# Decoder kernel, self attentions and wide cross attention: score matmuls and their PSUM banks rearranged

## What is computed

```python
# layer 1 self attention ("a1"): 16 heads of 8, rotary positions, masked by pages of 32 keys
scores = jnp.einsum('bqhd,bkhd->bhqk', q, k) * scale
scores = jnp.where(allowed[None, None], scores, jnp.finfo(scores.dtype).min)
out = jnp.einsum('bhqk,bkhd->bqhd', softmax(scores), v).reshape(B, T, E) @ wo
# layer 3 self attention ("a3"): 16 heads of 8, no mask, the same form
# layer 3 cross attention ("wide"): 16 heads of 64 over 154 context keys, with masks, then @ WO + bO
```

## Time and profile before

| | |
|---|---|
| median of 3 runs | 2627.68 us (2613.83 to 2633.36) |
| the profiled execution | 2624.98 us |
| its span | 2623.2 us, mean granted clock 0.866 |
| TensorE busy | 80% of the span |
| VectorE busy | 63% |
| ScalarE busy | 39% |

### The profile page before, as it was taken

How to read it: one execution, slowest core, us unless ns; L and a number is a source line. 1 busy time by engine, 2 the same in 40 slices (tenths; PEclk the granted TensorE clock), 3 DMA queues, 4 the chain that set the end, 5 groups by cost and what they waited for, 6 DMA issues and landing times. The chain is left out here.

```text
span 2623.2 us, 35892 instructions
## 1 busy us (share of the span) xinstructions
PE 2103.5 (80%) x11968; PEld 1397.2 (53%) x11992; DVE 1653.1 (63%) x4036; ACT 1028.7 (39%) x2290; POOL 542.7 (21%) x907
## 2 busy tenths in 40 slices
PE   7696999976998796557774995696699878988788
PEld 3354788853555455222332553585343346866677
DVE  5565677764674565569996455456688565555655
ACT  2353222211564452255551343321177633443333
POOL 0341111001110430148882330110211000000000
PEclk8597999986896797679996797798699879999989
DMA  8320000003110420000002310001311100000000
GB/s 316 92 61 16 1 1 1 1 16 106 41 51 21 110 54 1 0 0 1 0 0 88 77 45 7 0 1 42 120 49 41 27 31 1 0 0 0 0 1 17
DMA packets 60049, 94.43 MB, mean 36 GB/s; under 512 B 11313, under 2 KB 33137, under 8 KB 58737
## 3 DMA queue, kind: packets, MB, share of 16 engines
q1 hardware_dynamic: 29792, 55.57, 6.3%
q0 software_dynamic: 29952, 36.45, 5.8%
q10 hardware_dynamic: 144, 0.39, 0.1%
HBM read 65.63 MB, written 31.29 MB: 37 GB/s over the span
## 5 line engine op out<-in xcount | busy, mean ns | idle before, releaser
L904 DVE TENSOR_REDUCE m<-banks 128x1 f32<-128x512 f32 (+3 forms) x512 | 272.4, 583 | 76.7 <-PE banks L1057 50.0
L2435 PEld LDWEIGHTS banks<-w_ffn,eh 128*128 128x128 f32 x2144 | 279.2, 191 | 20.9
L2435 PE MATMUL banks<-w_ffn,eh 128*128 128x128 f32 x2144 | 280.8, 274 | 0.0
L1325 DVE TENSOR_REDUCE m<-banks 128x2 f32<-128x308 f32 x384 | 164.2, 475 | 173.5 <-PE banks L1604 97.9
L1025 ACT ACTIVATE p<-banks 128x512 f32<-128x512 f32 (+3 forms) x512 | 233.9, 522 | 98.4 <-PE banks L1103 58.8
L2423 PE MATMUL banks<-x_hi,w_hi 128*128 128x512 f32 x472 | 210.2, 445 | 18.8 <-PEq L330 18.8
L1055 PE MATMUL banks<-K,Qf 32*128 32x512 f32 (+2 forms) x512 | 180.7, 506 | 37.8 <-PEq L330 32.9
L2424 PE MATMUL banks<-x_lo,w_hi 128*128 128x512 f32 x472 | 188.5, 399 | 0.0
L2425 PE MATMUL banks<-x_hi,w_lo 128*128 128x512 f32 x472 | 187.7, 398 | 0.0
L2405 ACT ACTIVATE et<-banks 128x512 f32<-128x512 f32 x140 | 83.7, 598 | 246.9 <-PE banks L2425 246.9
L1101 PE MATMUL banks<-Q,K 32*128 32x512 f32 (+2 forms) x512 | 151.3, 492 | 15.0 <-ACT p L1025 13.1
(11 more groups left out here) (402 smaller groups left out, 4387.0 us busy)
## 6 DMA issues: line engine op xcount, KB each, us to landing
Qf<-stack_q_plain POOLq DMA_DIRECT2D x48, 256.0 KB, 3.0
Qf<-stack_q_masked POOLq DMA_DIRECT2D x32, 256.0 KB, 3.0
K<-stack_k_self POOLq DMA_DIRECT2D x32, 256.0 KB, 3.1
w_ffn<-ffn_dram SPq DMA_DIRECT2D x1, 6144.0 KB, 36.0
stack_q_plain<-q_hi SPq DMA_DIRECT2D x24, 256.0 KB, 3.5
stack_q_masked<-q_hi SPq DMA_DIRECT2D x16, 256.0 KB, 2.9
stack_k_self<-k_hi SPq DMA_DIRECT2D x16, 256.0 KB, 3.2
K<-stack_k_ctx POOLq DMA_DIRECT2D x48, 80.0 KB, 2.7
```

What stands on the lines that cost most here:

```text
L904: ins = dve.reduce_max(k.m[:, t, h:h + 1], bank[:, 0:(t + 1) * P if k.kind == "page" else S], AX)
L1325: dve.reduce_max(k.m[:, t:t + 2, h], first_banks[c % 3][:].rearrange("p (a k) -> p a k", a=2)[:, :, 0:S2], AX).then_inc(sem("max_done"), 1)
L2435: last = pe.matmul(bank[:, t * P:(t + 1) * P], k.h[:, n % RING, t * P:(t + 1) * P], w(down.format(e))[:, i * P:(i + 1) * P], start=(i == 0 ...
```

## The change

- Self attentions, first scores: banks 2 to 5 as two pairs; two consecutive chunks (two heads) fill a pair, one maximum of 128 x 2 x 512 reads both. TensorE waits once per pair, for the maximum of two pairs before. The result bank moves from 5 to 6.
- Self attentions, second scores: two banks (0, 1) in place of three; unit x waits for the exponential of unit x - 2.
- Wide: `kk` holds each pair of heads once, without zeros; each head has a score matmul of its own over its 64 rows and 154 columns, the two heads of a pair in different banks; both masks after the four matmuls.
- Branches of `narrow_block` that no call reaches are removed.

```diff
-    score_banks, first_banks = tuple(ps[n] for n in SBANKS), tuple(ps[n] for n in FBANKS)
-    o_bank, misc = ps[5], ps[7]
+    score_banks, o_bank, misc = ps[0:2], ps[6], ps[7]
+    def first_pair(pair):
+        at = 2 + 2 * (pair % 2)
+        return net.banks[:, at:at + 2, :]
...
-                bank = first_banks[c % 3]
                 dve.wait_ge(sem("scores_done"), c + 1)
...
-                    ins = dve.reduce_max(k.m[:, t, h:h + 1], bank[:, 0:(t + 1) * P if k.kind == "page" else S], AX)
-                ins.then_inc(sem("max_done"), 1)
+                width = (t + 1) * P if k.kind == "page" else S
+                dve.reduce_max(k.m[:, t, h - 1:h + 1], first_pair(c // 2)[:, :, 0:width], AX).then_inc(sem("max_done"), 1)
...
-                maximum(c)
+                if c % 2 == 1:
+                    maximum(c)
...
-                    nc.scalar.activation(k.p[:, x % PBUFS, q0:S], score_banks[x % 3][:, q0:S], ACT.Exp).then_inc(sem("exp_done"), 1)
+                    nc.scalar.activation(k.p[:, x % PBUFS, q0:S], score_banks[x % 2][:, q0:S], ACT.Exp).then_inc(sem("exp_done"), 1)
...
-                if c >= 3:
-                    pe.wait_ge(sem("max_done"), c - 2)
+                if c >= 4 and c % 2 == 0:
+                    pe.wait_ge(sem("max_done"), c // 2 - 1)
...
-                bank, kt, j = score_banks[x % 3], u // GROUP, u % GROUP
+                bank, kt, j = score_banks[x % 2], u // GROUP, u % GROUP
...
-                if x >= 3:
-                    pe.wait_ge(sem("exp_done"), x - 2)
+                if x >= 2:
+                    pe.wait_ge(sem("exp_done"), x - 1)
...
-        self.kk = sb("kk", [P, HEADS, KPAD])
+        self.kk = sb("kk", [P, HEADS // 2, KPAD])
...
-            dve.memset(k.kk[:], 0.0)
...
-                dve.scalar_tensor_tensor(k.kk[:, 2 * c:2 * c + 2, 0:S2], over(ps[2 + c % 2][:, 0:S2], 1, 2), w("x3_bk")[:, c:c + 1],
-                                         over(w("halfsel"), 2, S2), ALU.add, ALU.mult).then_inc(sem("kk_ready"), 1)
+                dve.tensor_scalar(k.kk[:, c, 0:S2], ps[2 + c % 2][:, 0:S2], w("x3_bk")[:, c:c + 1], None, ALU.add).then_inc(sem("kk_ready"), 1)
...
+                for j in range(GROUP):
+                    c, rows = 2 * g + j // 2, slice(XHD * (j % 2), XHD * (j % 2 + 1))
+                    out = ps[2 * (n % 2) + j % 2][:, j // 2 * S2:(j // 2 + 1) * S2]
+                    pe.matmul(out, k.qT[rows, c, t * P:(t + 1) * P], k.kk[rows, c, 0:S2], start=j < 2, stop=False, skip_group_check=True)
                 for i in range(2):
-                    c = 2 * g + i
                     out = ps[2 * (n % 2) + i][:, 0:2 * S2].rearrange("p (h k) -> p h k", h=2)
-                    pe.matmul(out, k.qT[:, c, t * P:(t + 1) * P], k.kk[:, 2 * c:2 * c + 2, 0:S2], start=True, stop=False)
-                    pe.matmul(out, w("negi"), over(k.mq[:, t, 0:S2], 1, 2), start=False, stop=True).then_inc(sem("scores_done"), 1)
+                    pe.matmul(out, w("negi"), over(k.mq[:, t, 0:S2], 1, 2), start=False, stop=True, skip_group_check=True).then_inc(sem("scores_done"), 1)
```

More of the change, by code:

```diff
@@ L898, in maximum @@
                 h = GROUP * (n % GROUPS) + j
-                bank = first_banks[c % 3]
                 dve.wait_ge(sem("scores_done"), c + 1)
-                if ctx_keys:
-                    ins = dve.reduce_max(k.m[:, t:t + 2, h], bank[:].rearrange("p (a k) -> p a k", a=2)[:, :, 0:S2], AX)
-                else:
-                    ins = dve.reduce_max(k.m[:, t, h:h + 1], bank[:, 0:(t + 1) * P if k.kind == "page" else S], AX)
-                ins.then_inc(sem("max_done"), 1)
+                width = (t + 1) * P if k.kind == "page" else S
+                dve.reduce_max(k.m[:, t, h - 1:h + 1], first_pair(c // 2)[:, :, 0:width], AX).then_inc(sem("max_done"), 1)
             def minus_maxima(n):
-                dve.wait_ge(sem("max_done"), nch * (n + 1))
+                dve.wait_ge(sem("max_done"), nch // 2 * (n + 1))
                 if n >= 2:
@@ L1040, in first_scores @@
                 t, j = k.chunk(i)
-                rows, bank = slice(RG * j, RG * (j + 1)), first_banks[c % 3]
+                rows, bank = slice(RG * j, RG * (j + 1)), first_pair(c // 2)[:, c % 2]
                 if i == 0:
@@ L1044, in first_scores @@
                     pe.wait_ge(net.loaded_sem["K"][n % k.nks], came("K", n, k.nks))
-                if c >= 3:
-                    pe.wait_ge(sem("max_done"), c - 2)
[L1047 to L1057, removed]
-                last.then_inc(sem("scores_done"), 1)
[L1060 to L1067, removed]
+                if c >= 4 and c % 2 == 0:
+                    pe.wait_ge(sem("max_done"), c // 2 - 1)
+                width = max((t + 1) * P, FULLRATE) if k.kind == "page" else S
+                last = pe.matmul(bank[:, 0:width], k.Qf[rows, n % k.nq, t * P:(t + 1) * P], k.K[rows, n % k.nks, 0:width], start=True, stop=True)
+                if k.kind == "page":
+                    last = pe.matmul(bank[:, t * P:(t + 1) * P], w("pageq")[rows, :], w("pagek")[rows, :], start=False, stop=True, skip_group_check=True)
+                last.then_inc(sem("scores_done"), 1)
             def lower_queries(n):
@@ L1088, in second_scores @@
                 x = nun * m + u
-                bank, kt, j = score_banks[x % 3], u // GROUP, u % GROUP
+                bank, kt, j = score_banks[x % 2], u // GROUP, u % GROUP
                 if u == 0:
                     pe.wait_ge(sem("Q2_ready"), m + 1)
-                if x >= 3:
-                    pe.wait_ge(sem("exp_done"), x - 2)
[L1094 to L1105, removed]
+                if x >= 2:
+                    pe.wait_ge(sem("exp_done"), x - 1)
+                rows = slice(RG * j, RG * (j + 1))
+                q0 = kt * P if k.kind == "page" else 0
+                wide = min(q0, S - FULLRATE)
+                last = pe.matmul(bank[:, wide:S], k.K[rows, m % k.nks, kt * P:(kt + 1) * P], k.Q2[rows, m % 2, wide:S], start=True, stop=True)
+                if k.kind == "page":
+                    last = pe.matmul(bank[:, kt * P:(kt + 1) * P], w("pagek")[rows, :], w("pageq")[rows, :], start=False, stop=True, skip_group_check=True)
                 last.then_inc(sem("st_done"), 1)
-            def mask_second_scores(m, u):
-                pe.matmul(score_banks[(nun * m + u) % 3][:], w("negi"), (k.mr if u == GROUP else k.mt)[:, m // GROUPS, :], start=False, stop=True).then_inc(sem("st_done"), 1)
             def products(n, quad):
@@ L1164, in _ @@
                 first_scores(c)
-                if k.kind == "full":
-                    mask_first_scores(c)
             lower_queries(0)
@@ L1176, in _ @@
                             first_scores(chunks[at])
[L1177 to L1181, removed]
                     if ctx_keys:
@@ L1834, in maxima @@
                     dve.wait_ge(sem("scores_done"), 2 * n + i + 1)
-                    last = dve.reduce_max(k.m[:, n % 2, 2 * i:2 * i + 2], ps[2 * (n % 2) + i][:, 0:2 * S2].rearrange("p (h k) -> p h k", h=2), AX)
+                    last = dve.reduce_max(k.m[:, n % 2, i::2], ps[2 * (n % 2) + i][:, 0:2 * S2].rearrange("p (h k) -> p h k", h=2), AX)
                 ch.link(last)
```

2 lines of the change are left out of this document (1 added, 1 removed).

## The result

The changed kernel takes 2645.63 us (median of 5 runs, 2641.41 to 2652.85), the kernel before 2630.03 in the runs beside it: a ratio of 1.0078 with a 95% interval of 1.0046 to 1.0109. The medians are 16 us apart, the means, to which the ratio belongs, 20. Run again in a later experiment it came to 1.0101 (1.0068 to 1.0134). The forecast was no change beyond 1%, and the result is one, inside the stated 2603 to 2652 but near its upper end. The sum behind the forecast was +1, and it came out at +16 in the profiled executions (spans 2639.6 against 2623.2).

A forecast was written before the change was run, and what follows sets the result against it. TensorE's fixed order against the exponentials was taken to bound the self attentions, TensorE and VectorE the wide steps. 15 - 1 - 13 = +1 on 2624.98 gave 2626, as a median 2628; range 2603 to 2652.

The forecast's parts named there:

- Wide, -13: Wide attention: scores by halves of rows side by side, no zeroing, shorter key bias; 13 us less in all.
- Rival A: Wide scores: the halves do not overlap, first maximum later than 1.2 after the load; total 2648 to 2657; chance 0.15.
- Merged maxima worth nothing on the path: Self attentions: one double maximum saves VectorE at most 1.15 per group, but off the path.
- Rival B: Self attentions: VectorE sets the pace, so merged maxima gain and the longer wait is hidden; 2585; chance 0.11.
- a3, +15: a3 self attention: two banks cost 0.80 a group, 11 us for 14 groups, plus 4 for first and last groups.
- a pair then takes 3.23, four pairs 12.92: a3: unit 3 waits 0.49 longer, so a pair of steps goes from 2.74 to 3.23, a group from 12.12 to 12.92.
- Rival C: Self attentions: waits given back less, all of 0.49 in every a3 pair, a1 +5; total 2652; chance 0.08.
- a1, -1: a1 self attention: longer second-score waits against vanished first-score waits, -0.15 in a plain group; 1 us less in all.
- in the five or so groups at half clock, I take +0.3: a1: groups at half clock, where TensorE has less slack, were taken to lose 0.3 each.
- The bound of +31 for a1: a1, upper bound: 0.49 lost in every pair, 2.0 a group, +31 us.

The follow-up runs named there:

- the two matmuls: Changed kernel plus two unused 128-row matmuls of 512 columns, after a wait, in step 1 of every a1 group: 2629.96 us, ratio 1.0016 to the kernel before.
- the bare wait: Changed kernel plus only a wait for the double maximum before the first second score of step 1 in a1 groups: 2649.78 us, ratio 1.0091.
- the three-bank kernel with the products between: Kernel before plus the wide part, odd steps' products moved between the two second scores, result bank copied after unit 3: 2684.23 us, ratio 1.0243.

## Why the prediction was right, and where its steps were not

*Wide, -13: right.* The profiles give -12 in the loop and -3 ahead of it, the run of this part alone -11. The halves overlap, the change of tile form costs about what was taken (0.76 against 0.77 to the mask), the chain of VectorE starts at 1.10. Rival A needed a first maximum later than 1.2 and falls. The longer steps are at 3.82, forecast 3.7; before 4.00.

*Merged maxima worth nothing on the path: right.* With or without them a3's groups take 12.47 to 12.50 and the ratios agree (1.0182 and 1.0176). Rival B, VectorE as the pace, falls with it: it gives groups under 12.1. The first scores' wait for a maximum went, as expected; most of it went with the two banks alone (1.7 us in 130 of a3, longest 0.2; before 5.2 in 120, longest 0.5).

*a3, +15: the step wrong, the size met in this profile by luck.* The step "a pair then takes 3.23, four pairs 12.92" took the 0.56 from unit 3 to the products over from the old timeline. Measured is 0.43: in the new pattern the first score no longer starts after its second score but beside it (both at 2028.20). A pair is 3.09, a group 12.47; in whole groups the two banks cost 0.35, not 0.80. In this profile a3 with its last group still comes to 15.2 (12.7 + 2.5), since a part that the forecast did not have makes up for it: 7.6 us in the first two groups, at the lower clock. Some 6 of these are chance, as the repeat shows (second group 12.23 in place of 18.39); in six of the seven other profiles with this pattern the stretch takes +7. Rival C, all of 0.49 in every pair, falls, though its total of 2652 is near the time measured.

*a1, -1: wrong, by 17 us.* The arithmetic of a group at the full clock nearly held: 10.41 against 10.42, forecast 10.2 to 10.4. What failed is the term "in the five or so groups at half clock, I take +0.3". It fixed the number of groups at half clock as that of the trace before. The added waits leave TensorE paused for 0.57 us in step 1 (0.38 before), and the time at 1.2 GHz rises from 44 us to between 83 and 169 in executions of that order. That the clock is the cause, and that it hangs on what TensorE does there, is shown by the two matmuls that bring 21 us back while the bare wait brings nothing. The bound of +31 for a1 held it in this profile, for another reason than the one given; in the two later profiles of the same order a1 takes 34 and 46 us more than before, beyond it.

The total of +1 was thus wrong by about the a1 term. That the result still lies within the range is luck: its upper end was drawn for A and C, neither of which happened. The clock should have been a rival: a1 stood at 0.82 before the change, and its groups took 11.4 on average against 10.42 in a plain one. What the rows of before could not tell is that longer waits would bring more of it.

*Left open.* Whether the two matmuls work because they fill the pause, or because they drive all 128 rows where the scores drive 32 at a time, was not separated: a pause filled with matmuls of 32 rows was not tried. Why a3 keeps the full clock with pauses of up to 0.67 us, where a1 loses it with 0.57, is open too. Nor was it settled why the three-bank kernel with the products between stays at 1.2 GHz in a1 with hardly a gap showing on TensorE. And the clock differs between executions of the same kernel, in a1 (83 and 135 us at 1.2 GHz) and in a3's second group, so it can't be forecast for one execution.

## What to carry to other kernels

In a stretch whose mean granted clock is below 1, count a new wait of TensorE twice: once for its own length, and once for the chance that more of the stretch falls to 1.2 GHz, where each microsecond spent is about a third of one lost here. Such a loss doesn't show in groups at the full clock, so take groups at either clock apart before judging an edit, and look at a second profile of the same kernel before you give a group at the lower clock to the edit: here 6 us of a3 came and went between two profiles. Where a short pause can't be removed, matmuls that nobody uses may cost less than the pause; try them, and try the bare wait beside them.

## What the runs showed of the hardware

- More work made the kernel faster: 30 matmuls of 512 columns over 128 rows (two from the start of the first to the next score: 0.66 us at the full clock) turned 1.0101 into 1.0016; the same wait without them gave 1.0091. With such matmuls at the starts of the stages too, the first group's clock was 0.64 in a1 and 0.67 in a3, against 0.50 or 0.51 in the thirteen other profiles.
- A pause does not decide the clock alone: a3 kept 1.00 with pauses of up to 0.67 us in its groups, a1 lost it with 0.57.
- TensorE can show as busy for 229.95 of 233.16 us and be granted 0.54 of its clock all the same.
- Two executions of one kernel can have a different clock at the same place: the changed kernel's second a3 group took 18.39 us at 0.51 in one and 12.23 at 1.00 in the other.
- fp32 matmuls on rows 0 to 63 and 64 to 127 run side by side: eight of 154 columns in 0.80 us.
- A maximum over two PSUM banks in one instruction costs 1222 ns, against 1220 for the double maximum elsewhere and 2 x 682 for two single ones: a bank border costs nothing that shows.
